# Layer 2 attention with its q, k, v and output products in row halves, v made for four head pairs at a time, and a deeper weight ring in layer 2's experts

## The reference

```
x = x + s * g                      # end of layer 1
xn = layernorm(x)
# layer 2, the attention: 16 heads of 64
q, k, v = xn @ Wq, xn @ Wk, xn @ Wv          # 128 -> 1024 each
scores = q @ k.T + position_bias             # per head, 512 x 512, not scaled
hidden = softmax(scores) @ v
s = hidden @ Wo                              # 1024 -> 128
# layer 2, the feed-forward part: 8 experts, the top two per token
g = silu(sum of the two experts' gated MLPs, 128 -> 256 -> 128)
x = x + s * g
```

## Time and profile before

| what | us |
|---|---|
| median of three runs | 2299.41 |
| the three runs | 2297.05, 2299.41, 2302.90 |
| the profiled execution, its own time | 2292.72 |
| its span | 2290.6 |
| TensorE busy in the span | 1884.3 |
| VectorE busy | 1444.1 |
| ScalarE busy | 1184.1 |
| layer 2's attention, from its first product to its last | about 719 to 1630 |
| layer 2's experts, from the first load | about 1651 to 1767 |

### The profile page before, as it was taken

How to read it: one execution, slowest core, us unless ns; L and a number is a source line. 1 busy time by engine, 2 the same in 40 slices (tenths; PEclk the granted TensorE clock), 3 DMA queues, 4 the chain that set the end, 5 groups by cost and what they waited for, 6 DMA issues and landing times. The chain is left out here.

```text
span 2290.6 us, 45771 instructions
## 1 busy us (share of the span) xinstructions
PE 1884.3 (82%) x16214; PEld 1249.4 (55%) x16214; DVE 1444.1 (63%) x4134; ACT 1184.1 (52%) x2452; POOL 445.1 (19%) x528
## 2 busy tenths in 40 slices
PE   3433898666957999999999999999698169999988
PEld 3222896555944555555555555555487134544557
DVE  4677222463356777777777777777465656777725
ACT  1122453324635777777777767777232305666653
POOL 0055352034530111111110000000056210000000
PEclk9966999877978999999999999999899558999989
DMA  3131774025742000000000000001176232423101
GB/s 130 70 103 36 252 259 147 28 76 175 273 171 36 12 11 11 11 11 11 11 9 2 1 1 2 2 2 57 48 258 216 89 113 70 132 71 95 43 3 37
DMA packets 118811, 176.74 MB, mean 77 GB/s; under 512 B 16184, under 2 KB 76704, under 8 KB 118144
## 3 DMA queue, kind: packets, MB, share of 16 engines
q1 hardware_dynamic: 107248, 146.56, 20.0%
q0 software_dynamic: 10912, 22.53, 2.9%
q10 hardware_dynamic: 432, 4.79, 0.5%
HBM read 66.87 MB, written 43.62 MB: 48 GB/s over the span
## 5 line engine op out<-in xcount | busy, mean ns | idle before, releaser
L1883 ACT ACTIVATE t_p<-t_p,t_low 128x512 f32<-128x512 f32 x512 | 369.6, 722 | 259.2 <-DVE t_low L1954 253.0
L1954 DVE CUSTOM_DVE_ANT_0 t_p<-bank,L_skewed 128x512 f32<-128x512 f32 x512 | 332.0, 686 | 200.9 <-PE bank L1770 200.8
L2291 ACT ACTIVATE alibi_p<-pair 128x1024 f32<-128x1024 f32 (+1 forms) x192 | 168.1, 883 | 120.2 <-PE pair L2178 119.7
L2033 POOL COPY t_wide<-t_inverse 128x512 f32<-128x512 f32 x64 | 39.2, 612 | 809.8 <-DVE t_inverse L1970 801.6
L2350 DVE CUSTOM_DVE_ANT_0 alibi_junk<-bank,alibi_later 128x512 bf16<-128x512 f32 (+1 forms) x256 | 150.5, 622 | 62.2 <-PE bank L2190 59.4
L1785 PEld LDWEIGHTS pair<-ident,t_p 64*128 64x128 f32 x4096 | 168.5, 139 | 36.7 <-ACT t_p L1883 1.6
L1785 PE MATMUL pair<-ident,t_p 64*128 64x64 f32 x4096 | 169.3, 222 | 0.4 <-ACT t_p L1883 0.3
L1770 PEld LDWEIGHTS bank<-t_k_hi,t_q_hi 64*128 64x128 f32 x512 | 47.7, 183 | 162.6 <-issue 100.2
L1770 PE MATMUL bank<-t_k_hi,t_q_hi 64*128 64x512 f32 x512 | 128.4, 498 | 4.8 <-DVE t_low L1954 4.4
L1798 PE MATMUL pair<-t_pT,t_v 128*64 128x512 f32 x512 | 123.8, 603 | 9.7 <-DVE t_hT L1977 9.7
L1798 PE MATMUL pair<-g,t_v 128*64 128x512 f32 x512 | 124.0, 604 | 8.6 <-DVE t_hT L1977 8.6
(11 more groups left out here) (541 smaller groups left out, 4358.6 us busy)
## 6 DMA issues: line engine op xcount, KB each, us to landing
L0moe_w<-L_packed SPq DMA_DIRECT2D x43, 578.0 KB
L2moe_w<-L_skewed SPq DMA_DIRECT2D x43, 450.0 KB, 3.1
L1moe_w<-L_packed SPq DMA_DIRECT2D x27, 578.0 KB, 3.7
alibi_q_aug<-aug_q SPq DMA_DIRECT2D x8, 1024.0 KB, 7.5
alibi_k_aug<-aug_k SPq DMA_DIRECT2D x8, 1024.0 KB, 7.6
L_skewed<-bias_table SPq DMA_DIRECT2D x16, 448.0 KB, 9.5
slots<-g ACTq DMA_DIRECT2D x3, 1560.0 KB, 9.8
L0shared_rows<-answers SPq DMA_DIRECT2D x8, 512.0 KB, 4.3
```

The costliest lines, as they stand in the source:

```text
L1883: nc.scalar.activation(p[:, u % RING, :], p[:, u % RING, :], ACT.Exp, bias=low[:, u % 16:u % 16 + 1], scale=-1.0, accum_out=sums[:, n % 2, ...
L1954: nc.vector.tensor_tensor_reduce(out=p[:, u % RING, :], in0=score_ps[h][:], in1=skewed[:, (n % PAIRS) * 2 + h, start:start + SEQ], scale=- ...
L2291: nc.scalar.activation(p[:, u % P_RING, :, 0:w], flip_ps[u % 2][:, :, 0:w], ACT.Exp).then_inc(expd, 1)
```

## The change

In `t5_attention_block`:

- q and k are each two products of 64 rows, which add up in PSUM. `qk_first(n)` does the first half of q's rows and the second half of k's; after a group of transposes `qk_second(n)` does the other two. They stand in iteration n-1 between scores(n-1,1), turns(n-1,0) and scores(n-1,2). TensorE waits for its own first pair by a semaphore (`qk_begun`).
- v is made for four pairs at a time (512 columns of Wv), one tile of 128 tokens per step, four steps ahead; v of the first four steps is made at the start, into four banks that are free then. The halves of v's product are paired with the halves of `output`: `vo_first(n)` before turns(n,2), `vo_second(n)` after it.
- v for two groups of four pairs needs as much room as x; it takes x's place. x is stored to DRAM in the routing block by SP, read back at the end of the attention block, and layer 3's addition waits for that.
- The cuts by VectorE go: ScalarE copies q and k from PSUM to fp32r itself, and VectorE subtracts that.
- In VectorE's order `norm` comes before `move` in t = 0; `low_q` is in t = 1. On ScalarE `high_q` is in t = 0, `high_k` before the move in t = 1. On TensorE turn_scale comes before mix(n-1,1) and follows transposes.

In `sorted_experts_block` the ring of weights is six deep where the experts are gated (layer 2 alone).

```diff
-    DEEP, ROW_DEEP, AT_DEEP, AHEAD = 4, 6, 8, 2
+    DEEP, ROW_DEEP, AT_DEEP, AHEAD = 6 if gated else 4, 6, 8, 2
...
+        if keep_x:
+            @block.sync
+            def _(sp):
+                for b in range(k.NB):
+                    sp.dma_start(cols(k.x_dram, b), tiles(k.x, b)).then_inc(k.x_kept, 16)
...
-        v = st.sb("v", [P, 2, TPS, P])
+        v = k.x[:].rearrange("p t d -> p (t d)").rearrange("p (g t w) -> p g t w", g=2, t=TPS)
...
+            def q_half(n, h):
+                weight = wq[rows[h], (n % PAIRS) * P:(n % PAIRS + 1) * P]
+                x = k.xnT[rows[h], (n // PAIRS) * SEQ:(n // PAIRS + 1) * SEQ]
+                return nc.tensor.matmul(qv_ps[:], weight, x, start=(h == 0), stop=(h == 1))
...
+            def qk_first(n):
+                pe.wait_ge(v_ready, v_count(n - 1))
...
+                q_half(n, 0)
+                k_half(n, 1).then_inc(qk_begun, 1)
+
+            def qk_second(n):
+                pe.wait_ge(qk_begun, n)
+                q_half(n, 1).then_inc(q_made, 1)
+                k_half(n, 0).then_inc(k_made, 1)
+
+            def first_products():
+                nc.tensor.matmul(qv_ps[:], wq[:, 0:P], k.xnT[:, 0:SEQ], start=True, stop=True).then_inc(q_made, 1)
+                nc.tensor.matmul(kc_ps[:], wk[:, 0:P], k.xnT[:, 0:SEQ], start=True, stop=True).then_inc(k_made, 1)
                 for t in range(TPS):
+                    nc.tensor.matmul(first_v[t], k.xnT[:, t * P:(t + 1) * P], wv[:, 0:SEQ],
+                                     start=True, stop=True).then_inc(v_made, 1)
+
+            def v_half(n, h):
+                g, t = n // GROUP + 1, n % GROUP
...
+                return nc.tensor.matmul(qv_ps[:], k.xnT[rows[h], at:at + P], wv[rows[h], side:side + SEQ],
+                                        start=(h == 1), stop=(h == 0))
...
+            def vo_first(n):
+                if n >= 2:
+                    pe.wait_ge(normed, n - 1)
...
+                    ins = out_half(n - 2, 0)
+                if n + GROUP < STEPS:
+                    pe.wait_ge(q_low, n + 2)
+                    ins = v_half(n, 1)
...
             for n in range(STEPS + 2):
-                live = n < STEPS
+                live, ahead = n < STEPS, n + 1 < STEPS
                 if live:
                     scores(n, 1)
+                if ahead:
+                    qk_first(n + 1)
+                if live:
                     turns(n, 0)
-                if n + 1 < STEPS:
-                    q_product(n + 1)
-                    k_product(n + 1)
+                if ahead:
+                    qk_second(n + 1)
                 if live:
                     scores(n, 2)
                     turns(n, 1)
@@
                 if live:
                     scores(n, 3)
+                vo_first(n)
+                if live:
                     turns(n, 2)
+                vo_second(n)
+                if ahead:
+                    scores(n + 1, 0)
+                if live:
+                    turns(n, 3)
+                if 1 <= n <= STEPS:
+                    turn_scale(n - 1)
                 if n % PAIRS == 2 and n >= PAIRS and n < STEPS:
                     turn_sum(n // PAIRS - 1)
                 if 1 <= n <= STEPS:
                     mix(n - 1, 1)
-                if n + 1 < STEPS:
-                    scores(n + 1, 0)
-                if live:
-                    turns(n, 3)
-                if n >= 2:
-                    output(n - 2)
-                if 1 <= n <= STEPS:
-                    turn_scale(n - 1)
-                if n + 1 < STEPS:
-                    v_product(n + 1)
...
             def high_q(n):
-                act.wait_ge(q_cutted, n + 1)
+                act.wait_ge(q_made, n + 1)
...
-                nc.scalar.copy(q_hi[:, n % 2, :], q_cut[:]).then_inc(q_high, 1)
+                nc.scalar.copy(q_hi[:, n % 2, :], qv_ps[:]).then_inc(q_high, 1)
...
+            def store_first_v(t):
+                act.wait_ge(v_made, t + 1)
+                if t == 0:
+                    act.wait_ge(k.x_kept, 16 * NB)
+                nc.scalar.copy(v[:, 0, t, :], first_v[t]).then_inc(v_ready, 1)
...
+            sp.wait_ge(mixed, STEPS)
+            for b in range(NB):
+                sp.dma_start(tiles(k.x, b), cols(k.x_dram, b)).then_inc(k.x_in[b], 16)
```

More of the change, by code:

```diff
@@ L306, in gather, with norm_block @@
     k.n_got[b] += 16
-def norm_block(k, name, combine, router=None, logits=None, keep=None, top=0, stage=None, bias=None):
+def norm_block(k, name, combine, router=None, logits=None, keep=None, top=0, stage=None, bias=None, x_again=False):
     nc, NB = k.nc, k.NB
@@ L498, in _, with route_block @@
                 route(NB - 1)
-def route_block(k, name, logits, bias, top, kind, rows, layer, table=None):
+def route_block(k, name, logits, bias, top, kind, rows, layer, table=None, keep_x=False):
     nc, T, E = k.nc, k.NT, EXPERTS
@@ L1741, in k_product, with k_half @@
+            def k_half(n, h):
+                weight = wk[rows[h], (n % PAIRS) * P:(n % PAIRS + 1) * P]
+                x = k.xnT[rows[h], (n // PAIRS) * SEQ:(n // PAIRS + 1) * SEQ]
+                return nc.tensor.matmul(kc_ps[:], weight, x, start=(h == 1), stop=(h == 0))
+            def qk_first(n):
+                pe.wait_ge(v_ready, v_count(n - 1))
+                if (n - 1) % PAIRS == 3 and n - 1 >= PAIRS:
+                    pe.wait_ge(s_stored, (n - 1) // PAIRS)
                 if n >= 3:
@@ L1742, in k_product @@
                     pe.wait_ge(scaled, n - 2)
-                elif n >= 1:
+                else:
                     pe.wait_ge(k_low, n)
[L1745 to L1753, removed]
-                for t in range(TPS):
-                    at = (n // PAIRS) * SEQ + t * P
-                    ins = nc.tensor.matmul(qv_ps[:, t * P:(t + 1) * P], k.xnT[:, at:at + P], weight, start=True, stop=True)
-                ins.then_inc(v_made, 1)
+                q_half(n, 0)
@@ new lines, in v_half, with out_half @@
+            def v_half(n, h):
+                g, t = n // GROUP + 1, n % GROUP
+                at = (g * GROUP // PAIRS) * SEQ + t * P
+                side = g * GROUP % PAIRS * P
+                return nc.tensor.matmul(qv_ps[:], k.xnT[rows[h], at:at + P], wv[rows[h], side:side + SEQ],
+                                        start=(h == 1), stop=(h == 0))
+            def out_half(n, h):
+                return nc.tensor.matmul(out_ps[:], wo[rows[h], (n % PAIRS) * P:(n % PAIRS + 1) * P], hT[rows[h], :],
+                                        start=(n % PAIRS == 0 and h == 0), stop=(n % PAIRS == PAIRS - 1 and h == 1))
@@ new lines, in vo_first, with vo_second @@
+            def vo_first(n):
+                if n >= 2:
+                    pe.wait_ge(normed, n - 1)
+                    if (n - 2) % PAIRS == 0 and n >= 3:
+                        pe.wait_ge(summed, (n - 2) // PAIRS)
+                    ins = out_half(n - 2, 0)
+                if n + GROUP < STEPS:
+                    pe.wait_ge(q_low, n + 2)
+                    ins = v_half(n, 1)
+                if n >= 2 or n + GROUP < STEPS:
+                    ins.then_inc(vo_begun, 1)
+            def vo_second(n):
+                pe.wait_ge(vo_begun, n + 1)
+                if n >= 2:
+                    out_half(n - 2, 1).then_inc(added, 1)
+                if n + GROUP < STEPS:
+                    v_half(n, 0).then_inc(v_made, 1)
@@ L1797, in mix @@
                     for h in range(2):
[L1798 removed]
+                        ins = nc.tensor.matmul(mix_ps[rows[h], :], v[:, n // GROUP % 2, j, n % GROUP * P + h * HALF:n % GROUP * P + (h + 1) * HALF], pT[n % 2][:, h, j, :],
                                                start=(j == 0), stop=(j == TPS - 1))
[L1800 to L1801 removed]
+                ins.then_inc(mixed if half == 1 else half_mixed, 1)
             def turn_scale(n):
@@ L1807, in turn_scale @@
                      k.ident).then_inc(scale_made, 1)
[L1809 to L1814, removed]
             def turn_sum(b):
@@ L1901, in _ @@
             high_k(0)
-            store_v(0)
             exponents(0, 0, 0)
             exponents(0, 0, 1)
+            for t in range(TPS):
+                store_first_v(t)
             for n in range(STEPS + 1):
@@ L1910, in _ @@
                             exponents(m, s, 0)
+                        if t == 1 and n + 1 < STEPS:
+                            high_k(n + 1)
                         move(n, t)
@@ L2002, in _ @@
                             bias(m, s, 1)
+                    if t == 0 and n >= 2:
+                        norm(n - 2)
+                    if t == 1 and n + 1 < STEPS:
+                        low_q(n + 1)
+                    if n < STEPS:
                         move(n, t)
```

88 lines of the change are left out of this document (35 added, 53 removed).

## The result

The median before was 2298.23 us (four runs), after it 2237.27 us (2233.42 to 2238.8, four runs). Medians and ratios leave out the one execution that ran in a slower state, the profiled one of experiment three (2288.96 us, mean granted clock 0.897). The profiled execution has a span of 2235.6 us against 2290.6, so 55.0 us of the difference can be followed from one trace to the other.

A forecast was written before the change was run, and what follows sets the result against it. TensorE's own order of work was taken to bound layer 2's attention. Step 13.95 to 13.14 us, -51 over 63 steps, start +2, experts -2: -51 from 2299.4 gives 2248 us; own range 2234 to 2275.

The forecast's parts named there:

- (d): Attention step: TensorE's idle time before the mix, waiting on VectorE's norm, goes; 0.34 us saved per step.
- (a): Attention step: q, k, v, output as four pairs of row halves take 3.48 us, not 3.87; 0.39 saved.
- (b): Attention step: scores and transposes each meet another shape twice, not four times; 0.20 and 0.16 us saved.
- (c): Attention step: the turned scale, now between transposes and mix, pays its own shape changes; +0.18 us.
- (e): Attention step: new waits of TensorE in the new order; +0.10 us per step, bounds 0 and 0.6.
- The walk: New order timed with old durations: at turns(n,1) TensorE arrives at 3.75 us, ScalarE's exponent chain ends at 3.77.
- Start and tail: Attention's first and last steps: v of four pairs delays the start, +2 us (0 to 4); tail nothing.
- x out and in: x stored in routing, read back at attention's end: costs nothing, up to +4 us if issues hold the block's end.
- The experts: Layer 2's experts: ring of six weight buffers instead of four, -2 us, bounds -3.8 and 0.
- the second rival: Attention pairs: records in order, only half overlap, +0.91 us per step, 2356 us; chance 0.11 with its no-overlap extreme.
- The first rival: Attention: pairs work but ScalarE becomes late at turns(n,1) and (n,3); step 13.74, 2286 us; chance 0.07.
- The third: Attention: transposes next to 64-row products cost shape changes of their own; +0.72 us a step, 2293 us; chance 0.06.

The follow-up runs named there:

- experiment three: The changed kernel with q and k as full 128-row products again, between turns(n,0) and scores(n,2): 2268.35 us, ratio 0.9840.
- experiment two: The kernel before, with only VectorE's norm put ahead of its move in quarter 0: 2285.82 us, ratio 0.9927.
- experiment eight: The changed kernel with VectorE's norm back behind its move and reciprocal: 2238.08 us, ratio 0.9734.
- experiment four: The changed kernel with q, k, output and v all full 128-row products again: 2275.73 us, ratio 0.9891.
- experiment six: The changed kernel with one more ScalarE copy (512 columns) per step, between its first move and the second exponent: 2268.31 us, ratio 0.9860.
- experiment five: The changed kernel with a ring of four weight buffers, not six, in layer 2's experts: 2248.87 us, ratio 0.9778.
- experiment one: The changed kernel with both halves of each pair in the same 64 rows: 2433.14 us, ratio 1.0571.
- experiment seven: The changed kernel with both mix halves one behind the other after turns(n,1): 2329.57 us, ratio 1.0151.

## Why the prediction was right, step by step

**The stall (d).** Predicted -0.34, measured -0.32 by experiment two. The prediction named two reasons, norm's place and the cuts that are gone. Either is enough without the other: the place in experiment two (with the cuts), and in experiment eight the new kernel without the place. There the missing cuts and TensorE's new order act together; the cuts by themselves were not tried.

**Pairs abreast (a).** Predicted 3.48 us for four pairs. From the rows of the changed kernel: 0.87 (1100.58 to 1101.45), 0.85 (1106.81 to 1107.66), and for the second of each kind the way to the next transposes less a score group of 0.71 us: 1.61 - 0.71 = 0.90 and 1.60 - 0.71 = 0.89. Together 3.51.

**Fewer changes (b) and the turned scale (c).** Predicted -0.36 and +0.18. The transposes next to a pair take 0.49 and 0.50 us, those next to the mix or the turned scale 0.59 and 0.60; scores after a pair have no 0.10 to pay. The turned scale takes 0.58, where it had 0.43: +0.15. (a), (b) and (c) were -0.57 together; from 13.63 (only the order changed) to 13.04 the runs show -0.59. Experiments three and four split it otherwise: the new order with full shapes costs +0.10 against experiment two (the turned scale's 0.15 is in it), and the row halves then bring -0.34 and -0.35.

**The new waits (e): a term that was mis-sized.** Predicted +0.10, measured nothing: without it the forecast of the step is 13.04, which is what came. The walk said that the second exponent is ready at 3.77 and TensorE at 3.75 (the exponent's terms, as they are listed, add up to 3.72). In the changed kernel the two come at 3.74 and 3.77, so both times were right to 0.05 us, but the need was put too early: only the second half of the 16 transposes reads that exponent. The slack is not zero but 0.17 us (experiment six), and the 0.10 makes 6.3 us over 63 steps.

**What the step's sum left out.** Every eighth step also turns the sum of a block. It cost 0.97 us over the others before (14.92 to 13.95) and costs 0.44 now (13.48 to 13.04). It stood between transposes and mix, with a change of shape on each side, and waited for VectorE's copy; now it stands beside the turned scale, in the same shape, and waits for nothing. Seven such steps give 3.7 us that the prediction had not counted.

**Start and tail.** Predicted +2. The start, answering to the earlier trace rows:

```profile
724.38 1.10 PE L1774 MATMUL bank<-xnT,L_wq 128*128 128x512 f32 x2 [0.88 <-PEq L509]
...
726.17 3.60 PE L1777 MATMUL pair<-L_wv,xnT 128*128 128x512 f32 x8
729.70 0.51 PE L1821 MATMUL bank<-t_k_hi,t_q_hi 64*128 64x512 f32 x2
```

The four v take 3.5 us and scores(0,0) begin 5.32 us after q (forecast 5.4, before 4.15). To the first exponent it is 1.2 us more than before, and the tail behind the last step's first exponent is 2.6 us longer (26.9 against 24.3), so +3.8. Two things were mis-sized. The tail was put at nothing ("nothing is given back"); in experiment four, where output and v are full products, it is 24.5 us, and in experiment three, where only q and k are, 26.9, so the 2.6 us are what the halves of output cost without a partner. And turns(0,0) start 11.5 us after q (735.90) where they started 7.3 after it, 4.2 us later instead of 2.3; TensorE waits there for ScalarE's copies of v (the 1.9 us in the list above). The first three steps gain nothing by it: 38.9 us together, before 38.2, where the forecast had them 2.4 shorter. With these 3.1 us, which the steps below contain, the start costs 4.3 us and not 2.

**x out and in.** Predicted 0, from the earlier trace rows. SP's queue in the changed kernel:

```profile
698.98 9.45 SPq L554 DMA_DIRECT2D x_kept<-x  x8
...
1577.84 3.69 SPq L2066 DMA_DIRECT2D x<-x_kept  x8
```

They are issued until 708.4, 16 us before the attention's first q; the last issue ends at 1581.5, beside TensorE's last turned sum (1582.1). The gap from the last turned sum to the experts is 21.1 us, as before (21.2).

**The experts.** Predicted -2 (between -3.8 and 0), this trace -2.2, and by all traces about -3.5. The number came, the account behind it only in part: the waits for weights are gone, but as much waiting came up on the gathered rows, and the gain stands in TensorE's busy time (experiment five).

**The sum.** Between the two traces: steps -58.4 (63 distances, 882.1 to 823.7 us), start and tail +3.8, experts -2.2, unchanged stages -3.7, later start +5.5: together -55.0. The forecast had -51 for the steps; the other 7.4 are the 6.3 of (e) and the 3.7 of the turned sum, less 3.1 that the first three steps did not gain, and 0.5 that the last ones gained beyond their share (12.7 to 12.9 us each). The profiled execution missed its forecast (2241.7) by 4.3 us. Of the 10.7 us by which the median missed, the other 6 are scatter: the forecast put the median 6.7 us above the profiled execution, and for the changed kernel the two are equal. The start of the attention alone scatters by 7.7 us.

**The rule and the second rival.** In the changed kernel's trace q's second record and k's second start together at 1101.02, a product's own first record having started 0.43 us earlier; three slots of 0.43 would have put the transposes at 1.29 us and not at 0.87. No partner was held up. And where output has no partner any more, starts leave the order of the program:

```profile
1552.83 0.65 PE L1788 MATMUL pair<-t_hT,L_wo 64*128 64x512 f32 x1
...
1553.17 0.49 PE L1821 MATMUL bank<-t_k_hi,t_q_hi 64*128 64x512 f32 x1
1553.31 0.59 PE L1788 MATMUL pair<-t_hT,L_wo 64*128 64x512 f32 x1
```

A score product, later in the program, starts in the free rows at 1553.17, before output's second record at 1553.31. The Trainium skill, "TensorE: Matmul & The Clock Gate" (Part 3, packing small matmuls), states that matmuls start and end strictly in program order. Starts in this trace do not agree; ends are modelled, so nothing is said of them. The sentence near the top, that each engine executes its own instructions in order, is too strong for TensorE: starts in different row halves leave that order. The first rival (ScalarE late) did not come about; experiment six makes it, and that took 0.5 us more of ScalarE at one place. The third (changes between transposes and products in 64 rows) is refuted by the transposes at 0.49 us.

## What to carry to other kernels

A full product between neighbours of 64 rows can be cut into two row halves, each abreast with a half of another product in the other rows and another bank. That costs the same time on the array and saves the changes of shape (0.35 us per two products here); where no other product is left to pair with, it costs more (2.6 us in the tail); without the overlap (experiment one against the full shapes, 16.18 to 13.73) it costs 1.2 more instead. Before a chain is called tight, ask which record of a group needs it, and before a piece of work is moved away, ask whose turnaround it covers: moving 1.87 us of mix opened 1.2 us of waiting at a shared bank and 0.4 at the scores. A fix of order in the old schedule says nothing about the new one; try it there alone.

## What was not expected of the hardware

- Two row halves run their products apart from each other: a transpose started 0.42 us before the product that precedes it in the program (experiment one), but the free half does not run on as it likes. Six of its starts between 1104.30 and 1107.31 come 6 or 7 ns behind a record of the busy half, one with each, so the transposes' 16 records did not pass k as a whole (14 of the 16 start from 1105.16 on). By then it is three products ahead: a transpose starts at 1107.31, the scores of the other half before it in the program at 1107.33, 1107.97 and 1108.20.
- A pair of two-record products costs 0.85 to 0.90 us in two row halves and 1.7 in the same rows, against 0.95 to 0.99 for one full product with its change.
- A wait can hide in a group of records: 0.34 us per step in experiment six is in no list of waits, only in a length of 1.00 us where 0.66 is usual. Listed waits of TensorE are also too short, since they are counted from a modelled end: 1.02 us in the list is 1.18 by starts (experiment seven).
